# Last layer of a four-layer graph network: shift and weights issued earlier, value projections later, other PSUM banks, output block by block

## The chip, the cores and the metric

The kernel runs on one core of a Trainium2 chip. The metric is the device time of one execution in microseconds (us). The kernel is written engine by engine: TensorE (PE, matmuls), VectorE (DVE), ScalarE (ACT), GpSimd (POOL) and SyncE (SP, which issues the transfers) each run their own list of instructions in order, and wait on semaphores for one another.

## The reference

Four layers, each `x = x + layer(relu(layernorm(x)))`, over 1354 nodes of 256 features with one adjacency matrix. Only the last layer is touched:

```python
def _L3_gnn_ref(x, S, W, U):
    n = x.shape[0]
    S = S + jnp.eye(n, dtype=S.dtype)
    h = x @ W
    scores = h @ U @ h.T
    mask = S > 0
    scores = jnp.where(mask, scores, -jnp.inf)
    att = jax.nn.softmax(scores, axis=-1)
    att = att * mask.astype(att.dtype)
    S_tilde = S * att
    return S_tilde @ h
```

## The kernel before

The 1354 nodes make 11 blocks of 128 rows (the last has 74). Scores are held transposed: for a **group** of output nodes (512, 512 and 330 columns wide; blocks 0 to 3, 4 to 7, 8 to 10) there is one **tile** for each of the 11 blocks j of source nodes, so the layer has 33 tiles, numbered n = 11 * group + j. Each tile passes through this pipeline:

1. `score(n)` on PE: six matmuls (hi*hi, lo*hi, hi*lo, for two halves of the features) into one of two score banks (4, 5). Lines L252 to L254, called from L1327.
2. `add3(n)` on DVE (L1204): mask and score into the SBUF slot of the tile; this frees the score bank. `score(n)` waits for `add3(n-2)`.
3. `running(n)` on DVE (L830, L833): elementwise extreme over the 11 tiles of the group.
4. Once a group: `turn_max` on PE (L1351, transposes of the running extreme into a bank of `B3.shifts`), `top` on DVE (L812, reduction), `spread_max` on PE (L1360, the result spread over the partitions, in the same bank).
5. `shift(n)` on DVE (L841): the slot minus the spread extreme. It can't start before `spread_max` of its group.
6. `exp3(n)` on ACT (L733): exponential in place. For the first tile of a group a second exponential of the same slot goes to `total` first (L732).
7. `times_s(n)` on DVE (L1212): product with the adjacency tile into `w_ring`, a ring of three; it waits until tile n-3 has been aggregated.
8. `add_total(n)` on POOL (L400): sums the exponentials into `total`.
9. `aggregate3(n)` on PE (L1656): for each output block of the group one fp32 matmul of the weights with `v3`, accumulated over 11 tiles in a bank of its own (`B3.sums`, banks 0 to 3 for each group). Each shows as two matmul records, so a tile is 8 records (6 in the last group).
10. Once a group: `add_up` on PE (L1666, the column sums of `total`, into the shift bank), then `out3` on DVE (L1220 reciprocals, one for each block; L1224 scale and add to `x_sb`), then the transfer of each block to DRAM (L304, SP's queue, one for each block).

The value projections `values(b)` (PE, also L252 to L254, 256 columns) fill banks 1 and 2 and are copied to `v3` by ACT (L447). They have to be through before banks 1 and 2 take sums.

The order is written out by hand in loops over a step s. On PE, step s has `score(s)`, then `turn_max` at s = 11, 22, 33 and `spread_max` at 12, 23, 34, then `aggregate3(s - 15)`, then `add_up` at 25, 36, 47. `values` 0 to 7 are in steps 0 to 7, `values(8)` ahead of `make_t(2)` in step 9, 9 and 10 in step 10. On DVE step s has `top` (12, 23, 34), `out3` (26, 37), `add3(s)`, `shift(s - 13)`, `running(s)`, `times_s(s - 14)`; `out3(2)` comes behind the loop. `aggregate3` waits, at tiles 11 and 22, until `out3` of the group ahead has read all its sum banks (L1654 wait on `x_add[3]`).

Of the kernel before, what the change touches and what calls it, by code (L numbers as in the profile page):

```python
# [27 lines left out]
SLOTS3 = 18  # L28
RING = 3
# [19 lines left out]

def item_bank(kind, b):  # L50
    return ITEM_BANKS[ITEMS.index((kind, b))]
# [11 lines left out]
TURNED = [[2, 4, 1, 0] + [2, 4] * 3 + [2], [3] * NB, [7, 3] * 3 + [7] * 5, [3, 4] * 4 + [3, 0, 3]]  # L63
XB_BANKS, XA_BANKS = [4, 5, 6, 7], [0, 1, 2, 3]
# [8 lines left out]
def graph_layers_kernel(nc, x, adjT, wq, wk, wvT, wsa, wgcn, w2, w3, w3T, u3T, asa, cols, rws, eye, out):  # L73
    with ExitStack() as ctx:
# [160 lines left out]
        eye_add, w_set, tot_add, tot_mm = sem("eye_add"), sem("w_set"), sem("tot_add"), sem("tot_mm")  # L235
# [171 lines left out]
        def _(act):  # L407
# [300 lines left out]
            for s in range(NB):  # L708
# [31 lines left out]
        def _(dve):  # L740
# [452 lines left out]
            def add3(n):  # L1193
# [6 lines left out]
                if n >= SLOTS3:  # L1200
                    k = n - SLOTS3
                    dve.wait_ge(w_set, k + 1)
                    wait(dve, tot_add, 10 * (k // NB) + k % NB)
# [22 lines left out]

# [17 lines left out]
            for s in range(NB, NT + LAG - 1):  # L1244
                for gi in range(NG):
                    if s == NB * gi + 12:
                        top(gi, 1, ALU.min)
                    if gi < 2 and s == NB * gi + 26:
                        out3(gi)
                if s < NT:  # L1250
                    add3(s)
                if 13 <= s < NT + 13:
                    shift(s - 13, 1)
                if s < NT:
                    running(s, 1, ALU.min)
                if s >= 14:
                    times_s(s - 14)
# [4 lines left out]
        def _(pe):  # L1262
# [78 lines left out]
            def turn_max(gi, a):  # L1341
# [3 lines left out]
                if gi == 2:  # L1345
                    pe.wait_ge(s_sub[a], NB)
                    if a:
                        pe.wait_ge(rinv_set[1], PER)
# [295 lines left out]
            def aggregate3(n):  # L1644
# [7 lines left out]
                if n % NB == 0:  # L1652
                    wait(pe, x_add[3], last_of(gi - 1) if gi else 0)
                for b in blocks(gi):  # L1654
                    mine = slice((b % PER) * P, (b % PER) * P + rows(b))
                    ins = pe.matmul(ps[0:rows(b), B3.sums[b % PER], 0:D], w_ring[0:k, n % RING, mine], v3[0:k, j, :],  # L1656
                                    start=(j == 0), stop=(j == NB - 1))
                ins.then_inc(agg[1], 1)

            def add_up(gi):  # L1660

                pe.wait_ge(tot_add, 10 * (gi + 1))
                pe.wait_ge(s_sub[1], NB * (gi + 1))
                for b in blocks(gi):
                    k = b % PER
                    ins = pe.matmul(ps[0:rows(b), B3.shifts[gi % 2], k:k + 1],  # L1666
# [3 lines left out]
            for s in range(NT + LAG):  # L1670
# [11 lines left out]
                if s == 9:  # L1682
                    values(8, 1)
                    make_t(2, 1)
                if s == 10:
                    values(9, 1)
                    values(10, 1)
                for gi in range(NG):
                    if s == NB * gi + 11:
# [47 lines left out]
```

## Time and profile before

| | us |
|---|---|
| median of 3 runs | 442.11 |
| lowest, highest | 441.32, 442.44 |
| profiled execution | 442.61 |
| span of its instructions | 440.8 |
| PE busy | 409.3 (93%) |
| DVE busy | 325.4 (74%) |
| ACT busy | 217.4 (49%) |
| POOL busy | 88.5 (20%) |

The span runs from the first to the last instruction; 1.8 us of the profiled time lie outside it. Busy shares are averages over the whole kernel. The last layer's scores begin at about 313 us of the span, and its last transfer ends it. In the profile's tables "issue" is time in which an engine waited for nothing that the profile shows, and PEclk is the clock granted to TensorE, where 1.00 is 2.4 GHz and 0.50 is 1.2 GHz.

### The profile page before, as it was taken

The numbers are of one execution on the slowest core, as the hardware profiler recorded it, in microseconds if no ns is written. First come the engines' busy times: TensorE is split into PE (matmuls) and PEld (weight loads), VectorE is DVE, ScalarE is ACT, GpSimd is POOL, SyncE is SP. The second block draws the span as 40 slices with busy tenths as digits, with TensorE's granted clock in tenths as the row PEclk, the third lists the DMA queues.
The fourth block names the chain that finished last, engine by engine and source line by source line (L and its number), as shares of the span: only waits on it lengthen the run. The fifth ranks groups of instructions, "written<-read, shape, count | busy, mean of one in ns | idle before, by whom it ended". The sixth has DMA issues, their size and how long they took to land.

```text
span 440.8 us, 7365 instructions
## 1 busy us (share of the span) xinstructions
PE 409.3 (93%) x2556; PEld 363.2 (82%) x2556; DVE 325.4 (74%) x749; ACT 217.4 (49%) x446; POOL 88.5 (20%) x105
## 2 busy tenths in 40 slices
PE   8999999999998979999999998898799899999795
PEld 7788789999897969999999767797588788978674
DVE  5899798899865649879989361675467778768872
ACT  2342999955784657876867723124132212212230
POOL 1280000001101324220311020022000033424452
PEclk9999999999999999999999999899699999989989
DMA  8991000000000010000000000000000000010010
GB/s 258 381 372 43 1 1 1 1 0 2 1 1 1 1 49 1 2 0 3 1 0 1 1 1 0 1 1 1 0 1 1 0 0 1 1 49 1 5 45 31
DMA packets 10301, 13.96 MB, mean 32 GB/s; under 512 B 645, under 2 KB 7193, under 8 KB 10265
## 3 DMA queue, kind: packets, MB, share of 16 engines
q1 hardware_dynamic: 10264, 13.49, 9.0%
q8 instruction: 21, 0.34, 0.3%
q14 instruction: 16, 0.12, 0.1%
HBM read 12.10 MB, written 1.39 MB: 31 GB/s over the span
## 4 chain that ended last, share of the span: by engine, by line
PE 75%; DVE 15%; issue 6%; ACT 2%; POOL 0%; DVEq 0%; ACTq 0%; POOLq 0%
PE ps L1656 12%; PE ps L1378 9%; PE ps L1373 8%; PE ps L1374 8%; PE ps L252 6%; PE ps L254 6%; PE ps L253 6%; PE ps L1299 6%; PE ps L1612 4%; PE ps L1613 3%; PE ps L1269 2%; DVE m_sb L833 2%; PE ps L1397 1%; DVE s_sb L803 1%; PE ps L1565 1%
## 5 line engine op out<-in xcount | busy, mean ns | idle before, releaser
L1373 PE MATMUL ps<-v_hi,p_hi 128*128 128x258 f32 (+3 forms) x242 | 64.8, 298 | 1.1 <-DVE x_sb L859 0.7
L1656 PE MATMUL ps<-v,w_ring 128*128 128x256 f32 (+3 forms) x242 | 59.1, 395 | 4.8 <-DVE x_sb L1224 3.2
L1374 PE MATMUL ps<-v_lo,p_hi 128*128 128x258 f32 (+3 forms) x242 | 61.1, 282 | 0.0
L1656 PEld LDWEIGHTS ps<-v,w_ring 128*128 128x128 f32 (+3 forms) x242 | 45.9, 193 | 13.4 <-issue 3.7
L252 PE MATMUL ps<-mid_hi,big_hi 128*128 128x512 f32 (+2 forms) x132 | 54.0, 409 | 1.8 <-DVE big_lo L771 1.0
L253 PE MATMUL ps<-mid_lo,big_hi 128*128 128x512 f32 (+2 forms) x132 | 49.2, 373 | 0.0
L254 PE MATMUL ps<-mid_hi,big_lo 128*128 128x512 f32 (+2 forms) x132 | 49.1, 372 | 0.0
L319 POOL TENSOR_TENSOR mr_all<-mr_all,mhalf 128x4 f32<-128x4 f32 (+1 forms) x12 | 12.8, 1066 | 175.4 <-DVE mr_all L765 175.4
L400 POOL TENSOR_TENSOR total<-total,s_sb 128x512 f32<-128x512 f32 (+3 forms) x27 | 30.8, 1140 | 83.9 <-DVE w_ring L1212 83.9
L1373 PEld LDWEIGHTS ps<-v_hi,p_hi 128*128 128x128 f32 (+3 forms) x242 | 44.7, 185 | 3.5 <-ACT p_hi L453 1.6
L1374 PEld LDWEIGHTS ps<-v_lo,p_hi 128*128 128x128 f32 (+3 forms) x242 | 44.7, 185 | 0.5
L733 ACT ACTIVATE s_sb<-s_sb 128x512 f32<-128x512 f32 (+3 forms) x30 | 17.2, 574 | 50.8 <-DVE s_sb L841 50.8
L1378 PE MATMUL ps<-v_hi,p_lo 128*128 128x258 f32 (+3 forms) x242 | 40.4, 285 | 1.7 <-DVE p_lo L847 1.7
L841 DVE TENSOR_TENSOR s_sb<-s_sb,ps 128x512 f32<-128x512 f32 (+3 forms) x63 | 38.5, 611 | 0.0
L1378 PEld LDWEIGHTS ps<-v_hi,p_lo 128*128 128x128 f32 (+3 forms) x242 | 32.5, 185 | 2.8 <-DVE p_lo L847 2.5
L1204 DVE SCALAR_TENSOR_TENSOR s_sb<-adjT_sb,ps 128x512 f32<-128x512 f32 (+3 forms) x30 | 18.5, 618 | 21.9 <-PE ps L254 21.8
L833 DVE TENSOR_TENSOR m_sb<-m_sb,s_sb 128x512 f32<-128x512 f32 (+3 forms) x51 | 32.7, 640 | 0.6
L1373 PE MATMUL ps<-big_hi,mid_hi 128*128 128x258 f32 (+3 forms) x121 | 31.3, 290 | 1.9 <-ACT mid_hi L561 1.9
L356 POOL TENSOR_TENSOR mid_lo<-adjT_sb,mid_hi 128x512 fp32r<-128x512 f32 (+2 forms) x16 | 19.8, 1238 | 57.8 <-ACT mid_hi L561 57.8
L1374 PE MATMUL ps<-big_lo,mid_hi 128*128 128x258 f32 (+3 forms) x121 | 30.3, 282 | 0.0
L415 ACT ACTIVATE z_buf<-x_sb,mr_all 128x256 f32<-128x256 f32 x40 | 22.4, 591 | 14.7 <-POOL mr_all L322 14.7
L570 ACT ACTIVATE p_hi<-s_sb,minus_r 128x512 fp32r<-128x512 f32 (+3 forms) x33 | 22.2, 672 | 14.5 <-DVE s_sb L1023 7.4
(172 smaller groups left out, 984.7 us busy)
## 6 DMA issues: line engine op xcount, KB each, us to landing
adjT_sb<-in_adjT_dram SPq DMA_DIRECT2D x1, 2816.0 KB, 16.6
adjT_sb<-in_adjT_dram SPq DMA_DIRECT2D x3, 768.0 KB, 10.0
adjT_sb<-in_adjT_dram SPq DMA_DIRECT2D x1, 1815.0 KB, 20.9
out_dram<-x_sb SPq DMA_DIRECT2D x10, 128.0 KB
x_sb<-in_x_dram SPq DMA_DIRECT2D x2, 512.0 KB, 4.6
adjT_sb<-in_adjT_dram SPq DMA_DIRECT2D x1, 512.0 KB, 11.6
rows_sb<-in_rows_dram SPq DMA_DIRECT2D x1, 385.0 KB, 11.2
s_sb<-in_wq_dram SPq DMA_DIRECT2D x1, 256.0 KB, 3.9
```

The source lines that it names most:

```text
L252: eng.matmul(out_ap, lhs[0], rhs[0], start=first, stop=False)
L253: eng.matmul(out_ap, lhs[0], rhs[1], start=False, stop=False)
L254: return eng.matmul(out_ap, lhs[1], rhs[0], start=False, stop=last)
L400: pool.tensor_tensor(r, r, slot3(n), ALU.add).then_inc(tot_add, 1)
L415: act.activation(z_buf[:, b % 4, :], x_sb[:, b, :], ACT.Identity, bias=mr_all[:, b, 0:1], scale=mr_all[:, b, 1:2]).then_inc(zd, 1)
L833: dve.tensor_tensor(m, m, mine(n), op).then_inc(s_max[a], 1)
L841: dve.tensor_tensor(mine(n), mine(n), ps[0:rows(j), bank, 0:CW[gi]], ALU.subtract).then_inc(s_sub[a], 1)
L1299: ins = pe.matmul(out_ap, h_mid[:, b, c, 0:rows(b)], w[:, c, 0:n], start=(c == 0), stop=(last and c == C - 1))
L1373: pe.matmul(out_ap, left_[0][0:k, n % RING, mine], right_[0][0:k, j, 0:cols_], start=(j == 0), stop=False)
L1374: pe.matmul(out_ap, left_[0][0:k, n % RING, mine], right_[1][0:k, j, 0:cols_], start=False, stop=False)
L1378: ins = pe.matmul(ps[0:rows(b), banks[b % PER], 0:cols_], left_[1][0:k, n % RING, mine], right_[0][0:k, j, 0:cols_], start=False, stop=(j ...
L1656: ins = pe.matmul(ps[0:rows(b), B3.sums[b % PER], 0:D], w_ring[0:k, n % RING, mine], v3[0:k, j, :], start=(j == 0), stop=(j == NB - 1))
```

## The change

The order of the last layer's instructions is rewritten from step 9 on; the arithmetic is the same.

- **Value projections**: `make_t(2)` directly behind `score(9)`; `values(8)` between `turn_max(0)` and `spread_max(0)` in step 11, `values(9)` in step 12, `values(10)` in step 13, all behind the step's score. ACT copies them out alternating with `exp3(0)` and `exp3(1)`.
- **Shorter lags**: `shift(n)` in step n + 11 for the first group, n + 12 for the others (before: n + 13); `times_s(n)` one step later, `aggregate3(n)` two. So n + 13 and n + 14 for `aggregate3`, before n + 15. From step 22 on DVE's order in a step is `add3`, `running`, `times_s`, `shift`; up to there it stays `add3`, `shift`, `running`, `times_s`. At steps 11 and 12 it is written out.
- **Banks**: sums of the third group in banks 4, 5 and 7 (`SUMS3`) in place of 0 to 2. The column sums of `total` go to columns 256 and up of bank 3 in place of the shift bank. The third group's first aggregation waits for all scores and all shifts of the second group, no longer for `out3(1)`. The second group's first aggregation waits for `out3(0)` one block at a time.
- **Group ends**: `add_up(0)` behind `aggregate3(10)` in step 23, with no aggregation in step 24; `add_up(1)` behind `aggregate3(21)` in step 35. DVE does `times_s(11)` and `out3(0)` at the head of step 24, `out3(1)` at the head of step 37. `out3` has one reciprocal for the group.
- **Last output**: in `aggregate3(32)` the column sums come behind the first block's matmul, and `out3(2)` takes each block when its own matmul is done.
- **ACT**: `exp3` does the in-place exponential first; for the first tile of a group a copy of the result goes to `total`, behind a wait for it.

```diff
+LAG3 = 14
+def shift_step(n):
+    return n + (11 if n < NB else 12)
+def tiles_at(s, after):
+    return [n for n in range(NT) if shift_step(n) + after == s]
+SUMS3 = [[0, 1, 2, 3], [0, 1, 2, 3], [4, 5, 7]]
+TOTALS_BANK = 3
...
                 act.wait_ge(s_sub[1], n + 1)
+                act.activation(slot3(n), slot3(n), ACT.Exp, scale=-1.0 / TINY).then_inc(pf[1], 1)
                 if j == 0:
                     wait(act, tot_mm, gi - 1)
-                    act.activation(total[0:rows(j), gi % 2, 0:CW[gi]], slot3(n), ACT.Exp, scale=-1.0 / TINY)
-                act.activation(slot3(n), slot3(n), ACT.Exp, scale=-1.0 / TINY).then_inc(pf[1], 1)
-            for n in range(NT):
+                    act.wait_ge(pf[1], n + 1)
+                    act.activation(total[0:rows(j), gi % 2, 0:CW[gi]], slot3(n), ACT.Copy)
+            for b in range(8, NB):
+                values(b, 1)
+                exp3(b - 8)
+            for n in range(3, NT):
                 exp3(n)
...
             def out3(gi):
                 dve.wait_ge(tot_mm, gi + 1)
-                dve.wait_ge(agg[1], NB * (gi + 1))
+                if gi < 2:
+                    dve.wait_ge(agg[1], NB * (gi + 1))
+                b0, b1 = blocks(gi)[0], last_of(gi)
+                dve.reciprocal(rinv[:, b0:b1], ps[:, TOTALS_BANK, D:D + b1 - b0]).then_inc(rinv_set[1], 1)
+                dve.wait_ge(rinv_set[1], gi + 1)
                 for b in blocks(gi):
-                    r, bank = rows(b), B3.shifts[gi % 2]
-                    dve.reciprocal(rinv[0:r, b:b + 1], ps[0:r, bank, b % PER:b % PER + 1]).then_inc(rinv_set[1], 1)
-                for b in blocks(gi):
-                    r, bank = rows(b), B3.sums[b % PER]
-                    dve.wait_ge(rinv_set[1], b + 1)
+                    r, bank = rows(b), SUMS3[gi][b % PER]
+                    if gi == 2:
+                        dve.wait_ge(last_sum, b % PER + 1)
...
-            for s in range(NB, NT + LAG - 1):
-                for gi in range(NG):
-                    if s == NB * gi + 12:
+            add3(11)
+            top(0, 1, ALU.min)
+            shift(0, 1)
+            shift(1, 1)
+            add3(12)
+            times_s(0)
+            running(12, 1, ALU.min)
+            for s in range(13, NT + LAG3 - 1):
+                for gi in range(1, NG):
+                    if s == NB * gi + (12 if gi == 1 else 11):
                         top(gi, 1, ALU.min)
-                    if gi < 2 and s == NB * gi + 26:
-                        out3(gi)
+                if s == 24:
+                    times_s(11)
+                    out3(0)
+                if s == 37:
+                    out3(1)
                 if s < NT:
                     add3(s)
-                if 13 <= s < NT + 13:
-                    shift(s - 13, 1)
+                if s < 22:
+                    for n in tiles_at(s, 0):
+                        shift(n, 1)
                 if s < NT:
                     running(s, 1, ALU.min)
-                if s >= 14:
-                    times_s(s - 14)
+                for n in tiles_at(s, 1):
+                    if n != 11:
+                        times_s(n)
+                if s >= 22:
+                    for n in tiles_at(s, 0):
+                        shift(n, 1)
             out3(2)
...
-                if n % NB == 0:
-                    wait(pe, x_add[3], last_of(gi - 1) if gi else 0)
+                if n == 2 * NB:
+                    pe.wait_ge(s_add[1], NT)
+                    pe.wait_ge(s_sub[1], 2 * NB)
                 for b in blocks(gi):
+                    if n == NB:
+                        pe.wait_ge(x_add[3], b - PER + 1)
...
+                    if n == NT - 1:
+                        ins.then_inc(last_sum, 1)
+                        if b == 2 * PER:
+                            add_up(2)
...
                 if s == 9:
-                    values(8, 1)
                     make_t(2, 1)
-                if s == 10:
-                    values(9, 1)
-                    values(10, 1)
-                for gi in range(NG):
-                    if s == NB * gi + 11:
-                        if gi < 2:
-                            pe.wait_ge(t_lo[1], 2 * NG)
-                        turn_max(gi, 1)
-                    if s == NB * gi + 12:
-                        spread_max(gi, 1)
-                if s >= LAG:
-                    aggregate3(s - LAG)
-                for gi in range(NG):
-                    if s == NB * gi + 25:
-                        add_up(gi)
+                if s == 11:
+                    pe.wait_ge(t_lo[1], 2 * NG)
+                    turn_max(0, 1)
+                    values(8, 1)
+                    spread_max(0, 1)
+                if 12 <= s < 14:
+                    values(s - 3, 1)
...
+                for n in tiles_at(s, 2):
+                    aggregate3(n)
+                    if n == NB - 1:
+                        add_up(0)
+                    if n == 2 * NB - 1:
+                        add_up(1)
```

## Rows read from the trace of the kernel before

**Rows 1.** Who PE waited for from 330 us on (total, times, longest).
```profile
PE ps L1656 <- DVE x_sb L1224: 3.2, 2, 2.1
PE ps L1656 <- DVE w_ring L1212: 1.6, 1, 1.6
PE ps L1360 <- DVE mx L812: 0.6, 1, 0.6
```
**Rows 2.** Busy time of each engine by stretch, granted clock, DMA share, GB/s.
```profile
core 0: us, PE busy (x) PEld busy (x) DVE busy (x) ACT busy (x) POOL busy (x), PEclk, DMA share, GB/s
343.20:352.80 9.60, 8.04 (x40) 6.26 (x38) 7.18 (x13) 2.17 (x4) 0.00 (x0) 1.00 0.00 0
388.00:391.00 3.00, 3.00 (x9) 2.44 (x9) 1.75 (x4) 0.63 (x1) 1.12 (x1) 0.53 0.40 132
...
419.00:423.00 4.00, 3.92 (x11) 2.99 (x12) 3.46 (x7) 1.44 (x3) 2.10 (x3) 0.59 0.33 106
423.00:435.00 12.00, 12.00 (x58) 9.69 (x57) 6.17 (x13) 2.88 (x6) 6.75 (x8) 1.00 0.00 0
```
**Rows 3.** Timeline of PE, steps 9 to 12: start, us, operation.
```profile
338.56 0.32 PE L252 MATMUL ps<-big_hi,wa_hi 128*128 128x330 f32 x1
...
340.38 0.40 PE L252 MATMUL ps<-mid_hi,big_hi 128*74 128x512 f32 x1
...
341.79 0.28 PE L252 MATMUL ps<-wb_hi,big_hi 128*128 128x256 f32 x1
...
343.21 0.39 PE L252 MATMUL ps<-mid_hi,big_hi 128*128 128x512 f32 x1
...
344.61 0.60 PE L1351 MATMUL ps<-ident,m_sb 128*128 128x128 f32 x4
344.96 0.48 PE L252 MATMUL ps<-mid_hi,big_hi 128*128 128x512 f32 x1
```
**Rows 4.** Chain that ended last, in order of time: start, us, what.
```profile
352.82 1.99 PE ps L1656 x8
...
356.21 1.73 PE ps L1656 x8
...
384.98 0.80 PE ps L1666 x8
...
387.88 3.48 PE ps L1656 x8
...
392.43 1.73 PE ps L1656 x8
...
405.49 0.17 PE ps L254
...
416.19 0.80 PE ps L1666 x8
417.02 0.36 DVE rinv L1220 x4
...
419.08 16.07 PE ps L1656 x66
435.15 0.49 PE ps L1666 x6
435.66 0.29 DVE rinv L1220 x3
...
436.74 0.39 DVE x_sb L1224
```
**Rows 5.** Timeline of DVE: one step of group 0, then the tail.
```profile
346.65 0.69 DVE L1204 SCALAR_TENSOR_TENSOR s_sb<-adjT_sb,ps 128x512 f32<-128x512 f32 x1 [0.56 <-PE ps L254]
347.37 0.69 DVE L830 TENSOR_TENSOR m_sb<-s_sb 128x512 f32<-128x512 f32 x1
...
419.26 0.50 DVE L1212 TENSOR_TENSOR w_ring<-s_sb,adjT_sb 128x330 f32<-128x330 f32 x1
419.67 0.49 DVE L841 TENSOR_TENSOR s_sb<-s_sb,ps 128x330 f32<-128x330 f32 x1
```
**Rows 6.** Timeline of ACT: a value copy, exponentials of both widths.
```profile
343.41 0.38 ACT L447 ACTIVATE v<-ps 74x256 f32<-74x256 f32 x1 [0.32 <-PE ps L254]
...
354.00 0.63 ACT L733 ACTIVATE s_sb<-s_sb 128x512 f32<-128x512 f32 x1 [1.77 <-DVE s_sb L841]
...
420.20 0.48 ACT L733 ACTIVATE s_sb<-s_sb 128x330 f32<-128x330 f32 x1 [0.34 <-DVE s_sb L841]
```
**Rows 7.** Timeline of POOL: the last addition into `total`.
```profile
432.13 0.88 POOL L400 TENSOR_TENSOR total<-total,s_sb 74x330 f32<-74x330 f32 x1 [0.43 <-DVE w_ring L1212]
```

More of the change, by code:

```diff
@@ L234, in graph_layers_kernel @@
         p2_mm, h2hi, h2lo, mask2, agg2 = (sem(n) for n in ("p2_mm", "h2hi", "h2lo", "mask2", "agg2"))
-        eye_add, w_set, tot_add, tot_mm = sem("eye_add"), sem("w_set"), sem("tot_add"), sem("tot_mm")
+        eye_add, w_set, tot_add, tot_mm, last_sum = (sem(n) for n in ("eye_add", "w_set", "tot_add", "tot_mm", "last_sum"))
         def wait(eng, s, value):
@@ L1202, in add3 @@
                     dve.wait_ge(w_set, k + 1)
-                    wait(dve, tot_add, 10 * (k // NB) + k % NB)
+                    wait(dve, tot_add, 10 * (k // NB) + max(k % NB, 1))
                 dve.scalar_tensor_tensor(out=slot3(n), in0=adj_tile(n), scalar=0.0,
@@ L1651, in aggregate3 @@
                     h_done(pe, 3, NB)
-                if n % NB == 0:
-                    wait(pe, x_add[3], last_of(gi - 1) if gi else 0)
+                if n == 2 * NB:
+                    pe.wait_ge(s_add[1], NT)
+                    pe.wait_ge(s_sub[1], 2 * NB)
                 for b in blocks(gi):
+                    if n == NB:
+                        pe.wait_ge(x_add[3], b - PER + 1)
                     mine = slice((b % PER) * P, (b % PER) * P + rows(b))
-                    ins = pe.matmul(ps[0:rows(b), B3.sums[b % PER], 0:D], w_ring[0:k, n % RING, mine], v3[0:k, j, :],
+                    ins = pe.matmul(ps[0:rows(b), SUMS3[gi][b % PER], 0:D], w_ring[0:k, n % RING, mine], v3[0:k, j, :],
                                     start=(j == 0), stop=(j == NB - 1))
-                ins.then_inc(agg[1], 1)
+                    if n == NT - 1:
+                        ins.then_inc(last_sum, 1)
+                        if b == 2 * PER:
+                            add_up(2)
+                if n < NT - 1:
+                    ins.then_inc(agg[1], 1)
             def add_up(gi):
                 pe.wait_ge(tot_add, 10 * (gi + 1))
-                pe.wait_ge(s_sub[1], NB * (gi + 1))
+                if gi:
+                    pe.wait_ge(rinv_set[1], gi)
                 for b in blocks(gi):
                     k = b % PER
-                    ins = pe.matmul(ps[0:rows(b), B3.shifts[gi % 2], k:k + 1],
+                    ins = pe.matmul(ps[0:rows(b), TOTALS_BANK, D + k:D + k + 1],
                                     total[:, gi % 2, k * P:k * P + rows(b)], ones[:, 0:1], start=True, stop=True)
                 ins.then_inc(tot_mm, 1)
-            for s in range(NT + LAG):
+            for s in range(NT + LAG3):
                 if 6 <= s <= 8:
@@ L1682, in _ @@
                 if s == 9:
+                    make_t(2, 1)
+                if s == 11:
+                    pe.wait_ge(t_lo[1], 2 * NG)
+                    turn_max(0, 1)
                     values(8, 1)
[L1684 to L1687, printed above, removed]
-                for gi in range(NG):
-                    if s == NB * gi + 11:
-                        if gi < 2:
-                            pe.wait_ge(t_lo[1], 2 * NG)
-                        turn_max(gi, 1)
-                    if s == NB * gi + 12:
-                        spread_max(gi, 1)
-                if s >= LAG:
-                    aggregate3(s - LAG)
-                for gi in range(NG):
-                    if s == NB * gi + 25:
-                        add_up(gi)
+                    spread_max(0, 1)
+                if 12 <= s < 14:
+                    values(s - 3, 1)
+                if s == 22:
+                    turn_max(1, 1)
+                if s == 23:
+                    spread_max(1, 1)
+                if s == 33:
+                    turn_max(2, 1)
+                if s == 34:
+                    spread_max(2, 1)
+                for n in tiles_at(s, 2):
[4 more added lines that the diff above has]
+                        add_up(1)
 _INS = ["x", "adjT", "wq", "wk", "wvT", "wsa", "wgcn", "w2", "w3", "w3T", "u3T", "asa", "cols", "rows", "eye"]
```

2 lines of the change are left out of this document (removed).

## The prediction

> **What bounds the kernel now.** I read the busy shares first: PE is busy 93% of the span, so only time in which PE stands still or runs slowly can be won without removing matmuls, and this change removes none (the last layer's scores, aggregations, transposes and projections are all still there). Then the list of whom PE waited for in the last layer [rows 1]: 3.2 us on `out3` in two waits (ahead of tiles 11 and 22), 1.6 us on the first `times_s`, 0.6 us on `top`. Then the chain that ended last [rows 4], which is PE nearly throughout, so that excess can be read as actual time minus work at the usual pace. Last the granted clock by stretch [rows 2]: it is 1.00 (2.4 GHz) except behind those two waits, 0.53 from 388 to 391 and 0.59 from 419 to 423, which is the 1.2 GHz level for most of them. So each of the two `out3` waits costs about twice what the list of waits shows.
>
> **Pace of the pieces**, from start to start on PE [rows 3] and from the chain [rows 4]. `score` 1.40 us at 512 columns (343.21 to 344.61); `make_t(2)` 1.82 (338.56 to 340.38), which is twelve matmuls of 330 columns, 0.152 each, so a `score` of 330 columns, six of them, is 0.92 with its first one's start. Two `values` 1.42 (341.79 to 343.21), so 0.71 each. Four transposes 0.44, three 0.33 by proportion. An aggregation 1.73 with four blocks and 1.29 with three (three quarters). `add_up` 0.80, and 0.49 for the last. On DVE, one operation after another starts after 0.60 at 512 and 0.41 at 330 columns [rows 5]; an operation that needs the result of the one directly ahead starts after 0.72 at 512 (346.65 to 347.37), so I take 0.53 at 330. Between engines: 0.20 from the last score matmul's slot to the DVE or ACT instruction that reads it (343.21 to 343.41) [rows 3, 6], 0.03 between DVE and ACT, 0.05 from DVE to PE (times as the chain has them).
>
> **Part 1, front of the layer: 0.65 us won.** Before, the first aggregation starts at 352.82 with scores 0 to 15 issued. New, on the same clock: `score(9)` from 336.45, `make_t(2)` to 339.66, scores 10 and 11 to 342.46. `turn_max(0)` has to wait for `running(10)`: score 10 ends at 341.07, DVE starts at 341.27, dependent `running` 0.72 later, its result at 342.68; 0.3 us of wait. `values(8)` to 343.87 covers most of `top`, which ends at 344.03; 0.2 us of wait; `spread_max` to 344.50, `score(12)` to 345.90, `values(9)` to 346.62, `score(13)` to 348.02, `values(10)` to 348.74. Aggregation 0 needs `values(10)` in SBUF: ACT starts 0.20 later and takes 0.38 [rows 6], so 349.38 and a wait of 0.64. Its `times_s(0)` is done by 347.4 (`shift(0)` 344.70, exponential 345.41 to 346.04, `times_s` behind `add3(12)` at 346.70) and `exp3(1)` in front of the ACT copy ends at 347.8, so neither is late. Before, less two scores: 352.82 - 2.79 = 350.03. Won 0.65: the wait of 1.7 us is replaced by three that add up to 1.1. The bounds are 1.7 (no new wait) and 0 (each a third of a microsecond longer). The copy to `total` in place of the exponential costs the same 0.6 us on an ACT that is idle most of the time; the in-place exponential coming first takes 0.6 us from the path of tiles 0, 11 and 22.
>
> **Steady steps: nothing.** PE takes 3.12 us a step (1.40 + 1.73) against 2.4 on DVE (four operations), and `times_s` still stands one step ahead of its aggregation. From step 22 PE has 2.65 and DVE 0.53 + 0.41 + 0.60 + 0.60 = 2.14. The reordering there leaves `times_s(n)` behind `add3` and `running`, 1.4 us behind its `shift`; the exponential needs 0.71 + 0.66 = 1.37 (0.63 of it the exponential) [rows 6]. If DVE comes late, all of the 2.14 has to fit, and it does.
>
> **Part 2, group 0 to group 1: 2.3 us won.** Before: from `add_up(0)` at 384.98 to tile 12's aggregation at 392.43 PE does 0.80 + 1.73 + 2 x 0.92 = 4.37 us of work in 7.45, an excess of 3.08 [rows 4]. New: `add_up(0)` is followed by scores 24 and 25 (1.84 us), which cover `out3(0)`: reciprocal from +0.18, first block's `x_add` at about +0.8, then one every 0.41, and PE asks for them from +1.84, one every 0.43. That wait is gone. What is late next is `times_s(12)`. Queued on DVE behind `out3(0)`, with t = 0 where PE starts aggregation 11: `add3(24)` 0.2, `running(24)` 0.7, `shift(12)` 1.1, `add3(25)` 1.7, `running(25)` 2.25, `times_s(12)` 2.65, result 3.4. PE has aggregation 11 and score 26 in front: 2.65. So a new wait of 0.74, once; a step later DVE has caught up. Net 3.08 - 0.74 = 2.34. Bounds for that wait: 0 and 1.1.
>
> **Part 3, group 1 to the end of the aggregations: 3.5 us won.** Before, from score 32's last matmul at 405.66 (405.49 + 0.17) to 435.15 are 29.49 us. The work is aggregations 17 to 21, 5 x 1.73 = 8.65; two sets of three transposes 0.66; `add_up(1)` 0.80; 11 x 1.295 = 14.24; together 24.35. Excess 5.14: 1.2 up to `add_up(1)` (`turn_max(2)` and `spread_max(2)` wait, since `top(2)` stands behind a `times_s` that waits for the ring), 2.09 for `out3(1)`, 1.83 of slow clock behind it. New: sums in banks 4, 5, 7 take the `out3(1)` wait away, and `top(2)` stands ahead of its step's `times_s`. I laid the steps out from score 32's end as 0: aggregations 18 from 0, 19 from 2.06, 20 from 4.12, 21 from 5.85, `add_up(1)` 7.58, tile 22 from 8.38, 23 from 9.67; `top(2)` at 2.3, `times_s(21)` ready at 5.81, `times_s(22)` at 7.3. No wait up to there, one by a hair. Then two new ones. `out3(1)` sits ahead of `times_s(24)` on DVE: 8.99 + 0.18 + 4 x 0.41 = 10.82, ready at 11.37, PE free at 10.97: 0.40. And from there on `shift(n)` comes directly ahead of `times_s(n)` with nothing between, so the loop shift to exponential (0.49 + 0.03), exponential to `times_s` (0.48 + 0.03), `times_s` to next shift (0.41) takes 1.45 us a tile against PE's 1.295: 8 tiles x 0.155 = 1.24. Net 5.14 - 1.64 = 3.50. Bounds: the loop is 1.29 (PE's, hidden) to 1.6, so 4.7 to 2.3.
>
> **Part 4, the end: 0.5 us won.** Before, start of aggregation 32 to the end of the last `x_add`: 1.29 + 0.16 + 0.49 + 0.02 + 1.47 = 3.43 (433.70 to 437.13) [rows 4]. New, the column sums stand behind the first block's matmul and wait for POOL's last addition: `times_s(32)` is 0.05 older than aggregation 32, POOL starts 0.13 later and needs 0.88 [rows 7], so `add_up(2)` starts at 1.0 in place of 0.43. Then 0.49, two blocks 0.86, drain 0.2, last `x_add` 0.4: 2.97. Won 0.46; without the POOL wait it would be 1.0. Before, POOL was hidden since PE was three tiles behind; the exponential loop takes that cover away. The three last transfers come as before, 0.4 us apart, and the last needs the same 3.7 us from `x_add` to the end of the span.
>
> **Sum.** 0.65 + 2.34 + 3.50 + 0.46 = 6.95 us. Against the profiled 442.61 (which is 0.5 above the median): 435.7; against the median 442.11: 435.2. I take 435.4.
>
> **The clock.** The trace has three waits of PE of like size and two outcomes: 1.7 us ahead of 352.82 left the clock at 1.00 (343.20 to 352.80, PE busy 8.04 of 9.60) [rows 2], while 1.08 us ahead of 387.88 and 2.1 us ahead of 419.08 were each followed by about 3 us at 1.2 GHz; both of these stood close behind an `add_up`, eight matmuls of one column. The Trainium skill, page "TensorE: Matmul & The Clock Gate", Part 1, says that the activity window is free-running and does not reset with the work, so that how many matmuls run cold differs between runs of one kernel. By that a wait of given length can go either way, and the two outcomes here agree. The sum above has no drop left.
>
> **Rivals.** (A) One drop of the clock stays, behind the 0.74 us wait at tile 12 or behind `add_up(1)` and the 0.40 us wait. It costs what the chain shows [rows 4]: 3.48 - 1.73 = 1.75 for one aggregation plus 0.2 for the score behind it. Gives 437.3. For: the same neighbourhood as before. Against: waits are a third of the old ones, with dense scores between. Chance 0.2. (B) DVE and ACT hand over sooner than I took, or DVE stays ahead, so that the tail is PE's: 1.24 + 0.5 more, 433.7. Against: both durations are in the rows. Chance 0.12. (C) Both drops stay and the front wins nothing: 435.4 + 3.7 + 0.65 = 439.8, or with the loop at 1.6 another 1.2, 441.0. Chance 0.07. (D) Slower: in the tail PE stops briefly at each tile; if that takes the clock to 1.2 GHz and holds it there, a tile costs 2.59 in place of 1.45, for 10 tiles 11.4 us: 446.8. It decides at about 6 such tiles. Against: before, at 1.2 GHz the clock came back within 3.5 us under full load, and a slow PE is a busy PE. Chance 0.03. (E) The change doesn't act: aggregation 22 still waits, since one of its new conditions is as late as `out3(1)` was. By the layout all scores and shifts of group 1 are done 2.7 us ahead. Chance 0.03, about 439.
>
> **How the numbers follow.** My forecast has 0.55. The range leaves out (D) and most of (C): 433.3 (B with a little more) to 438.9 (A and a lost front). A measurement of this kernel can tell about 0.3%, 1.3 us, from no change. Faster by more than that holds for the forecast, A, B, E and most of C: 0.93; within: 0.04; slower: D and what I overlooked, 0.03.
>
> **What would show it.** Right: no wait of L1656 on `x_sb` L1224; granted clock 1.00 from 385 to the end of the aggregations; last layer's aggregations 25 to 32 at 1.45 us each, with DVE's L1212 waiting for ACT's L733; a wait of L1656 on `w_ring` near tile 12 of 0.7 us and of about 0.6 us of L1666 on POOL in the last tile. Wrong: tiles at 1.29 us (then the loop is shorter than I took), a clock of 0.5 anywhere in the layer behind its start, or a first aggregation later than 349.4.

## The result

The changed kernel takes 437.42 us (median of 4 runs, 435.35 to 438.10); beside it the kernel before took 442.27 (median of 4, 441.32 to 443.16). These medians differ by 4.9 us, 1.1%; the ratio on record is 0.987 with a 95% interval of 0.984 to 0.991, so the kernel is faster. Ratios leave out the few slow executions, those over 1.5% above the fastest of their kernel; medians take in all. Over all later comparisons the kernel before had a median of 443.1 (23 runs in the largest of them), and a second set of the changed kernel gave 437.33 and a ratio of 0.986, which is 5.8 us. The forecast was 435.4, 6.7 us less than before, in a range of 433.3 to 438.9.

| | before | after |
|---|---|---|
| median, us | 442.27 | 437.42 |
| profiled execution, us | 442.61 | 437.66 |
| span, us | 440.8 | 435.9 |
| start of score 9 | 336.45 | 337.61 |
| start of score 9 to the end of the last `x_add` | 100.68 | 94.57 |

The last row is the part that the change touches. Its start is worked out from the first matmul of `make_t(2)`, less one score (1.40) and, where `values(8)` stands between them, less another 0.71. In this part the change wins 6.11 us; 1.16 us of it are lost ahead of score 9, in code that it doesn't touch.

Who PE and DVE waited for in the last layer of the changed kernel (total, times, longest; PEld is the load of a matmul's stationary operand; L1686 is the aggregation, L1702 `add_up`, L1223 `times_s`, L737 the exponential, L411 POOL's addition):

```profile
DVE w_ring L1223 <- ACT s_sb L737: 7.1, 13, 0.7
...
PEld ps L1686 <- DVE w_ring L1223: 4.5, 11, 0.8
...
PE ps L1686 <- DVE w_ring L1223: 0.8, 2, 0.5
...
PE ps L1702 <- POOL total L411: 0.3, 1, 0.3
```

The row of the `out3` waits in [rows 1] is gone: no aggregation waits for `x_sb` any more. In its place stand `times_s` waiting 13 times for the exponential, and the aggregation's weight loads waiting 11 times for `times_s`. Busy time and granted clock by stretch (columns as in [rows 2]):

```profile
343.00:351.00 8.00, 7.23 (x43) 5.76 (x42) 6.76 (x12) 3.01 (x7) 0.00 (x0) 1.00 0.01 2
384.00:390.00 6.00, 5.52 (x33) 5.04 (x34) 5.81 (x13) 1.31 (x3) 0.19 (x1) 1.00 0.26 87
390.00:405.00 15.00, 15.00 (x80) 13.69 (x80) 13.16 (x25) 3.79 (x6) 7.52 (x7) 1.00 0.00 1
405.00:417.00 12.00, 12.00 (x64) 10.03 (x62) 9.52 (x20) 3.81 (x7) 5.97 (x5) 1.00 0.04 13
417.00:430.00 13.00, 12.44 (x52) 8.11 (x51) 7.56 (x17) 3.83 (x8) 7.97 (x9) 1.00 0.09 31
```

The clock is 1.00 throughout these stretches; [rows 2] had 0.53 and 0.59 behind the two waits. The chain that ended last, at the places of [rows 4]:

```profile
350.78 1.97 PE ps L1686 x8
...
383.88 0.80 PE ps L1702 x8
...
388.99 0.69 DVE w_ring L1223
389.73 1.99 PE ps L1686 x8
...
413.54 0.79 PE ps L1702 x8
414.32 1.42 PE ps L1686 x6
...
418.64 0.51 DVE s_sb L852
419.17 0.49 ACT s_sb L737
419.82 0.28 issue
420.10 0.50 DVE s_sb L852
420.62 0.49 ACT s_sb L737
...
427.55 0.90 POOL total L411
...
429.93 0.75 PE ps L1702 x6
430.70 0.19 DVE rinv L1231
430.92 0.88 DVE x_sb L1237 x2
```

Behind `add_up(1)` at 413.54 the next aggregation follows at once, where [rows 4] has 2.1 us of waiting for `out3`. Then the chain leaves PE and runs around the loop of `shift` (L852), exponential (L737) and `times_s`, 1.46 us a turn (418.64 to 420.10), and ends over POOL.

### The profile page after: what moved, and what is told of

Read it like the earlier page. It is cut to its first block, busy times and chain, and to the rows that moved or that the text cites. A ratio compares the mean times of both kernels' runs of the same rounds, so it can differ in the third digit from the quotient of the medians.

```text
span 435.9 us, 7356 instructions
## 1 busy us (share of the span) xinstructions
PE 409.0 (94%) x2556; PEld 360.6 (83%) x2556; DVE 323.3 (74%) x741; ACT 217.5 (50%) x446; POOL 87.9 (20%) x105
## 3 DMA queue, kind: packets, MB, share of 16 engines
q1 hardware_dynamic: 10264, 13.49, 9.0%
## 4 chain that ended last, share of the span: by engine, by line
PE 73%; DVE 15%; issue 6%; ACT 3%; POOL 1%; DVEq 0%; POOLq 0%; ACTq 0%
PE ps L1686 9%; PE ps L1405 9%; PE ps L1400 8%; PE ps L1401 8%; PE ps L263 6%; PE ps L265 6%; PE ps L264 6%; PE ps L1328 6%; PE ps L1639 4%; PE ps L1640 3%; PE ps L1298 2%; DVE m_sb L844 2%; PE ps L1424 2%; DVE s_sb L814 2%; PE ps L1592 1%
## 5 line engine op out<-in xcount | busy, mean ns | idle before, releaser
L1686 PE MATMUL ps<-v,w_ring 128*128 128x256 f32 (+3 forms) x242 | 58.0, 385 | 1.3 <-DVE w_ring L1223 0.8
L1686 PEld LDWEIGHTS ps<-v,w_ring 128*128 128x128 f32 (+3 forms) x242 | 43.2, 185 | 11.1 <-DVE w_ring L1223 4.5
L411 POOL TENSOR_TENSOR total<-total,s_sb 128x512 f32<-128x512 f32 (+3 forms) x27 | 30.5, 1131 | 80.3 <-DVE w_ring L1223 80.3
L737 ACT ACTIVATE s_sb<-s_sb 128x512 f32<-128x512 f32 (+3 forms) x30 | 17.3, 575 | 54.0 <-DVE s_sb L852 54.0
L852 DVE TENSOR_TENSOR s_sb<-s_sb,ps 128x512 f32<-128x512 f32 (+3 forms) x63 | 38.5, 612 | 0.8 <-PE ps L1387 0.7
L1034 DVE SCALAR_TENSOR_TENSOR s_sb<-s_sb,sx 128x512 f32<-128x512 f32 (+3 forms) x33 | 28.4, 859 | 1.2
```

The source lines that it names most:

```text
L411: pool.tensor_tensor(r, r, slot3(n), ALU.add).then_inc(tot_add, 1)
L852: dve.tensor_tensor(mine(n), mine(n), ps[0:rows(j), bank, 0:CW[gi]], ALU.subtract).then_inc(s_sub[a], 1)
L1034: dve.scalar_tensor_tensor(out=sum1(n), in0=left[0:rows(j), gi, 0:CW[gi]], scalar=sx[0:rows(j), j, 0:1], in1=sum1(n), op0=ALU.add, op1=ALU ...
L1686: ins = pe.matmul(ps[0:rows(b), SUMS3[gi][b % PER], 0:D], w_ring[0:k, n % RING, mine], v3[0:k, j, :], start=(j == 0), stop=(j == NB - 1))
```

## Experiments

All are read in two ways: by time, and by their own trace from the start of score 9 to the end of the last `x_add` (100.68 us before, 94.57 after). The second is what a wait or a slow clock in the last layer changes and nothing else, since the time ahead of score 9 differs between executions. How far a trace repeats can be read from the front: from score 9 to the first aggregation it is 16.34 to 16.37 us in all five kernels with the order of before, and 13.17 or 13.18 in the seven that have the changed front. By time the variants of the changed kernel can't be told from one another; what is said of them rests on one trace each. Each ratio is taken against executions of the kernel before that ran beside that kernel. Line numbers in rows of an experiment are its own. Where an expectation counts from the first aggregation, the changed kernel and its variants have two scores (2.79 us) more in that stretch than the kernel before and its variants.

| kernel | score 9 at | score 9 to last `x_add` | median us (runs) | ratio to before |
|---|---|---|---|---|
| before | 336.45 | 100.68 | 443.1 (23) | |
| changed | 337.61 | 94.57 | 437.42 (4) | 0.987 (0.984 to 0.991) |
| changed, again | 337.72 | 94.56 | 437.33 (4) | 0.986 (0.982 to 0.989) |
| before, banks alone | 336.77 | 98.83 | 440.98 (7) | 0.994 (0.991 to 0.996) |
| before, gap alone | 335.29 | 99.48 | 441.67 (12) | 0.997 (0.995 to 1.000) |
| before, waits filled | 338.79 | 99.23 | 442.61 (12) | 0.998 (0.996 to 1.001) |
| before, waits filled, half | 336.20 | 97.29 | 439.98 (12) | 0.993 (0.991 to 0.995) |
| changed, values back | 337.30 | 94.51 | 437.06 (2) | 0.987 (0.982 to 0.992) |
| changed, end back | 336.83 | 94.88 | 436.52 (2) | 0.986 (0.981 to 0.991) |
| changed, whole wait | 336.29 | 94.54 | 436.75 (2) | 0.986 (0.980 to 0.992) |
| changed, tail shift | 337.37 | 92.98 | 435.86 (5) | 0.983 (0.979 to 0.987) |
| best | 343.91 | 92.07 | 435.09 (6) | 0.981 (0.978 to 0.985) |
| best2 | 337.80 | 91.80 | 434.17 (4) | 0.981 (0.977 to 0.984) |

In the profiled execution of "best" the clock was at 0.50 from 260 to 270 us, ahead of the last layer, and its score 9 comes late; in its last layer the clock is 1.00.

### The changed kernel again

> The changed kernel once more, nothing altered: a second trace of it and more times. Theory: the last layer comes out the same to 0.1 us (first aggregation 13.17 us behind the start of score 9, tiles 25 to 32 at 1.46 us, last x_add 26.3 us behind the end of score 32), and what differs between executions lies ahead of score 9, which started at 337.61 us in the profiled execution of the changed kernel and at 336.45 in that of before, in code that neither touches. Rival: the 1.16 us ahead of score 9 belong to the change; then score 9 starts at 337.6 again.

Score 9 at 337.72, the same part 94.56 us: the last layer repeats to 0.01 us. By the one number named in the expectation the rival would stand. But all thirteen kernels have the same instructions ahead of step 9, and without "best" their score 9 starts between 335.29 and 338.79 in the five with the order of before and between 336.29 and 337.80 in the seven with the changed order. The 1.16 us lie well inside that, so I take them for scatter ahead of the last layer; twelve single traces don't rule out a small share of the change. The clock ahead of the last layer differs between executions too. Two stretches of the kernel before:

```profile
250.00:260.00 10.00, 8.97 (x52) 6.71 (x51) 7.47 (x27) 4.70 (x13) 2.81 (x6) 1.00 0.01 2
280.00:290.00 10.00, 10.00 (x77) 10.00 (x77) 8.42 (x28) 0.00 (x0) 0.74 (x1) 0.88 0.01 2
```

The same two of the changed kernel:

```profile
250.00:260.00 10.00, 8.99 (x44) 6.92 (x43) 6.86 (x25) 4.30 (x12) 2.08 (x4) 0.83 0.00 0
280.00:290.00 10.00, 8.74 (x73) 8.59 (x73) 9.22 (x29) 1.42 (x3) 0.00 (x0) 1.00 0.01 2
```

One execution has its slow clock at 280 us, the other at 250. That isn't where the 1.16 us come from, though: the changed kernel is up to 4.9 us behind at 255 us and back to 0.8 at 283. The 0.8 are there by 11 us of the span, and 0.3 to 0.4 more come between 312 and 319.

### Which part won it: banks alone

```diff
+SUMS3 = [[0, 1, 2, 3], [0, 1, 2, 3], [4, 5, 7]]
+TOTALS_BANK = 3
...
-                if n % NB == 0:
-                    wait(pe, x_add[3], last_of(gi - 1) if gi else 0)
+                if n == NB:
+                    wait(pe, x_add[3], last_of(gi - 1))
+                if n == 2 * NB:
+                    pe.wait_ge(s_add[1], NT)
+                    pe.wait_ge(s_sub[1], 2 * NB)
...
```

`out3`, `aggregate3` and `add_up` use these banks, and `add_up` waits for the reciprocals of the group ahead.

> The kernel before with the banks of the change alone: third group's sums in banks 4, 5, 7, totals in bank 3, aggregation 22 free of out3(1), nothing else moved. Theory (the wait is in DVE's order as much as in the bank): aggregation 22 starts 2.1 us earlier, at 417.0, but times_s(23) is queued behind out3(1) and is ready only at 419.8, so aggregation 23 waits 1.5 us and the clock falls as before: 0.5 us less than before, 441.6. Rival (the bank was the cause): the wait of 2.1 and the slow clock of 1.8 both go, 438.2.

1.85 us won in the trace, between the two expectations, and by time 0.6% (0.4 to 0.9). PE's timeline around aggregations 22 and 23 (start, us, engine, line, operation, idle before):

```profile
416.34 0.95 PE L1671 MATMUL ps<-ones,total 128*128 128x1 f32 x8
417.15 1.54 PE L1661 MATMUL ps<-v,w_ring 128*128 128x256 f32 x6
420.12 4.05 PE L1661 MATMUL ps<-v,w_ring 128*128 128x256 f32 x17 [1.43 <-DVE w_ring L1214]
```

The wait moved as the theory had it: aggregation 22 starts at once, and aggregation 23 waits 1.4 us since its `times_s(23)` is queued behind `out3(1)`. The bank by itself is worth 0.5 us there. What the theory missed is the clock: this time it stayed at 1.00 (2.88 of 4.00 us busy from 419 to 423, PEclk 1.00), behind a wait that is longer than the 1.07 us ahead of aggregation 11 in the same execution, behind which it fell (0.61 from 388 to 391). That is the other 1.3 us.

### Which part won it: the gap ahead of aggregation 11

```diff
-                if s >= LAG:
-                    aggregate3(s - LAG)
-                for gi in range(NG):
-                    if s == NB * gi + 25:
-                        add_up(gi)
+                n = s - LAG if s < NB + LAG else s - LAG - 1
+                if s >= LAG and s != NB + LAG:
+                    aggregate3(n)
+                    if n % NB == NB - 1:
+                        add_up(n // NB)
```

> The kernel before with one thing of the change: between add_up(0) and aggregation 11 PE does two scores (26 and 27) in place of one; aggregations 11 to 32 come one step later, lags on DVE, banks and the rest as before. Theory (a second score of 0.92 us is what covers out3(0), and with the wait goes the slow clock behind it): PE asks for x_add at 1.84 us behind add_up, all four blocks stand 1.97 behind it, so the wait falls from 1.08 to 0.15 and the clock stays at 1.00: 0.93 + 1.92 = 2.85 us less from the first aggregation to the last x_add, 81.5 in place of 84.31, and 440.3 in all; tile 22 still waits 2.1 and is slow behind it. Rival (out3(0) then delays times_s(12), as in the changed kernel, by 0.7): 82.2. Rival (the clock falls anyway): 83.4.

1.20 us won over the whole part, not 2.85. Up to `add_up(1)` it went as the theory says: from the first aggregation to `add_up(1)` 60.78 us (351.63 to 412.41) against 63.37 (352.82 to 416.19) before, 2.6 won; the wait for `x_sb` at aggregation 11 is 0.17 and the clock stays up. Behind the other wait, which is as long as before, 1.4 us of it are lost again:

```profile
415.31 17.49 PE ps L1656 x66
```

The same 66 records took 16.07 us in [rows 4]. The clock by single microseconds in this execution:

```profile
414.00:415.00 1.00, 0.00 (x0) 0.00 (x0) 1.00 (x3) 0.00 (x0) 0.00 (x0) 0.78 0.13 46
415.00:416.00 1.00, 0.69 (x2) 0.64 (x3) 1.00 (x4) 0.40 (x1) 0.00 (x0) 0.50 0.81 267
...
420.00:421.00 1.00, 1.00 (x4) 0.69 (x3) 0.13 (x1) 0.00 (x0) 0.00 (x0) 0.50 0.00 0
421.00:422.00 1.00, 1.00 (x5) 0.80 (x4) 0.79 (x2) 0.18 (x1) 0.54 (x1) 0.80 0.00 0
```

It was at 1.2 GHz for 7 us, under aggregations that ran without a break once they had started, against 3.3 us in the execution of [rows 2]. So what this variant wins in its first half is the wait and the slow clock together; the run doesn't part them.

### What the slow clock costs: waits filled with matmuls of no use

The second run has 4 and 8 matmuls in place of 8 and 16.

```diff
+                if n == NB:
+                    pe.wait_ge(s_add[1], 2 * NB + 4)
+                if n in (NB, 2 * NB):
+                    for _ in range(8 if n == NB else 16):
+                        pe.matmul(ps[:, 5 if n == NB else 4, 0:P], ident[:, :], ones[:, :], start=True, stop=True)
                 if n % NB == 0:
                     wait(pe, x_add[3], last_of(gi - 1) if gi else 0)
```

> The kernel before with matmuls of no use, 8 ahead of aggregation 11 and 16 ahead of aggregation 22, each 128 columns into a score bank that is free there; every wait is kept. Theory (the stillness of PE is what takes the clock to 1.2 GHz behind the out3 waits, and that costs as much as the waits): the clock stays at 1.00, aggregation 11 takes 1.75 in place of 3.48, tiles 22 to 24 take 1.3 each; from the first aggregation to the last x_add 80.7 us in place of 84.31, and 438.5 in all. Rival (the clock falls for another reason, such as what PE did before): 84.3 and 442.3; or it falls at one of the two: 82.5.

The clock stayed at 1.00 in both places, and aggregation 11 took 1.73 us. But I had sized the filling wrongly: a matmul of 128 fp32 columns takes 0.224 us, twice what I had assumed. Eight of them take 1.8 us in a wait of 1.08, sixteen 3.6 us in a wait of 2.1. What was left of the 3.7 us is 1.45 in the trace, and by time no difference can be told.

> As waits_filled with half the matmuls of no use: 4 ahead of aggregation 11 (0.9 us, the wait is 1.08) and 8 ahead of aggregation 22 (1.8 us, the wait is 2.09). waits_filled kept the clock at 1.00 but its matmuls took 0.224 us each, 0.7 and 1.6 us more than the waits that they fill. Theory: the clock stays at 1.00 with these too and nothing is added, so all of the slow clock's 3.75 us shows: 80.6 us from the first aggregation to the last x_add, 438.6 in all. Rival (the short stillness that is left is enough): one or both drops come back, 82.4 or 84.3.

With half of them:

```profile
387.00:390.00 3.00, 2.91 (x17) 2.51 (x17) 2.49 (x6) 0.63 (x1) 0.37 (x1) 1.00 0.53 175
416.00:419.00 3.00, 2.88 (x17) 2.39 (x17) 3.00 (x7) 0.96 (x2) 0.89 (x1) 1.00 0.53 175
```

3.39 us won with every wait of the kernel before in place, 0.7% by time (0.5 to 0.9). That the clock held isn't an accident of one trace: the mean clock over the whole execution was 0.987 or 0.991 in all 12 executions of this kernel, and 0.983 or less in 22 of the 23 of the kernel before that ran beside it. So of the excess at the two group ends about 3.4 us were the slow clock and 3.2 the waits. `add_up` by itself doesn't take the clock down, since it is still there; PE has to stand still as well. Whether standing still suffices isn't shown: every fall in the last layer had an `add_up` at most one score ahead of the wait. Of the two longer waits behind which the clock stayed up, the one ahead of the first aggregation (1.6 us) has no `add_up` near it, and that in banks alone (1.43) has an aggregation in between.

### The front: value projections back

`values(8)` to `values(10)` stand where they were before, on PE and on ACT; the lags are as changed.

> The changed kernel with the value projections 8 to 10, and ACT's copies of them, where they were before; lags, banks and the rest as changed. Read from score 9's start to the first aggregation, which is 16.37 us in the kernel before (13.58 less two scores) and 13.17 in the changed one. Theory (the front's gain comes from the shorter lag, the moved projections only trade one wait for another): PE waits 0.9 us for top between turn_max and spread_max with nothing over it, but no longer 0.35 for running(10) nor 0.5 to 0.8 for the copy of projection 10, so 13.0 to 13.3. Rival (the projections are what covers the waits): 13.9, the 0.9 us on top.

94.51 against 94.57 us, and 13.11 from score 9 to the first aggregation against 13.17: no difference worth naming. The wait is where the theory puts it:

```profile
345.44 0.60 PE L1379 MATMUL ps<-ident,m_sb 128*128 128x128 f32 x4
346.98 0.65 PE L1388 MATMUL ps<-ident,mx 128*128 128x128 f32 x4 [0.94 <-DVE mx L824]
```

PE stands 0.94 us between the two sets of transposes with no projection to do there, and gets it back at `turn_max` and at the first aggregation, where it no longer waits. Moving the projections is worth nothing. What remains for the front's gain is the shorter lag with the new order on DVE and ACT in steps 11 and 12; these two weren't tried apart.

### The end: sums behind all blocks again

```diff
-                    if n == NT - 1:
-                        ins.then_inc(last_sum, 1)
-                        if b == 2 * PER:
-                            add_up(2)
-                if n < NT - 1:
-                    ins.then_inc(agg[1], 1)
+                ins.then_inc(agg[1], 1)
+                if n == NT - 1:
+                    add_up(2)
...
```

`out3(2)` waits for the whole aggregation again.

> The changed kernel with the end as before: all three blocks' matmuls of tile 32, then the column sums, then out3(2) with no wait a block. Read from the start of tile 32's aggregation to the end of the last x_add: 3.21 us in the changed kernel, 3.43 in that of before. Theory: the sums then wait for POOL less (0.43 + 0.86 = 1.29 of cover against 1.0 needed, so not at all), and the end takes 3.4: 0.2 us longer than the changed kernel. Rival (block by block is worth the 0.86 of two blocks): 0.9 longer.

0.31 us longer over the whole part. In this trace tile 32's weights are ready at 428.10 and the last `x_add` ends at 431.71, 3.61 us; in the changed kernel 428.92 and 432.18, 3.26. So the last edit is worth 0.3 us, near what the theory gives and far from the 0.86 of two blocks: with the sums moved forward PE waits for POOL instead.

### The wait by block at aggregation 11

One wait for all four blocks of `out3(0)` in place of one a block.

> The changed kernel with aggregation 11 waiting for all four blocks of out3(0) before its first matmul, in place of one at a time. Theory (two scores cover out3(0) but for its last block): in the changed kernel aggregation 11 starts at 386.44 and the fourth x_add stands at 386.59, so PE waits 0.2 us, and that comes off the wait at tile 12 behind it: no change, 81.4 us from the first aggregation to the last x_add. Rival (the wait by block carries the gain at this place): 0.5 us or more longer, or the clock falls, 83.3.

94.54 against 94.57 us. Aggregation 11 starts 0.3 later and tile 12 waits 0.3 less. The two scores cover `out3(0)` but for its last block, and what waiting by block wins there is lost again at tile 12.

### The tail: shifts of the third group one step earlier

```diff
+EARLY = range(2 * 11 + 1, 3 * 11)
+def shifts_at(s):
+    return [n for n in range(NT) if shift_step(n) - (n in EARLY) == s]
...
                 if s >= 22:
-                    for n in tiles_at(s, 0):
+                    for n in shifts_at(s):
                         shift(n, 1)
```

> The changed kernel, with the shifts of the third group's tiles but its first one step earlier, nothing else. Theory (the loop shift, exponential, times_s, next shift sets the tail at 0.41 + 0.52 + 0.51 = 1.45 us a tile): with another tile's work between them the tail goes at PE's 1.30, 8 x 0.155 = 1.2 us won; the wait for out3(1) ahead of tile 24 stays (0.4), and PE falls far enough behind DVE that POOL's last addition is covered again, 0.6 won. Together 1.8 us less than the changed kernel, 435.6. Rival (PE itself takes 1.45 a tile in this stretch, or DVE is full): no change, 437.4.

1.59 us won. One tile's `shift` now follows the last at 1.33 us in place of 1.46, PE's pace:

```profile
417.64 0.48 DVE s_sb L857
...
418.97 0.45 DVE s_sb L857
```

and PE's aggregations from tile 22 on run without a break. So the loop was the bound of the tail in the changed kernel, as the theory has it. The total came near the 1.8 expected partly by luck, since two smaller parts of the theory were wrong and made up for each other. The wait at tile 24, which was to stay, went: its `shift` now stands ahead of `out3(1)`. And the wait for POOL, which was to go, stayed: POOL's third last addition took 1.49 us in place of 0.89 and the last `add_up` waited 0.39 for it. The traces of banks alone and of waits filled, half, have the same slow addition (1.48), and in all three DVE's last two `times_s`, which run beside it, take 1.59 together; in the next two kernels they take 2.31 and the addition 0.89. Why it is sometimes the one and sometimes the other that comes out longer stays open.

### A version that beats both

"Best" also makes the second group's shifts but the first one step earlier, and splits `out3(1)`:

```diff
-                if s == 37:
-                    out3(1)
+                if 37 <= s < 41:
+                    out3(1, s - 37)
```

> The changed kernel with three edits of DVE's order: all shifts but tiles 11 and 22 one step earlier from step 23 on, and out3(1) split into one block a step over steps 37 to 40. Theory: no wait of PE left from aggregation 11 to the end, so in addition to the 1.8 us of tail_shift the wait at tile 12 (0.5 to 0.7) and the one at tile 24 (0.4) go: 2.9 us less than the changed kernel, 434.5. Rival: moving the work only moves the wait (shift(12) ahead of times_s(11) delays out3(0)); then no better than tail_shift, 435.6.

2.50 us less than the changed kernel in the same part; `add_up(1)` is followed by 62 records in 13.49 us, ten tiles and a block without a wait. Of the 0.9 us beyond the tail shift 0.8 lie behind `add_up(1)`, where POOL's slow addition is missing here, so the split of `out3(1)` has little to show for itself. The wait at tile 12 stayed (0.5 us): `shift(13)` had taken `shift(12)`'s place in the queue.

> The kernel best with times_s(12) ahead of add3(25) on DVE, in step 24, nothing else. In best the wait at tile 12 stayed at 0.5 to 0.75, since shift(13) took the place of shift(12) in the queue. Theory: times_s(12) is then ready about 0.9 us ahead of PE and the wait goes: from the first aggregation to the last x_add 78.2 us in place of 78.90 (81.40 in the changed kernel, 84.31 before), 434.3 in all. Rival (add3(25), now 0.6 us later, holds up score 27): no change, 78.9.

0.27 us less than "best", not 0.7. Tile 12 waits no more; tile 13 does:

```profile
389.27 1.89 PE L1694 MATMUL ps<-v,w_ring 128*128 128x256 f32 x8
392.29 0.92 PE L1694 MATMUL ps<-v,w_ring 128*128 128x256 f32 x3 [0.21 <-DVE w_ring L1228]
```

`out3(0)` puts 1.8 us on DVE, which has only 0.5 us to spare in a step of 2.65. These orders chose the tile that pays; none of them let all go free. This version is at 434.17 us, ratio 0.981 (0.977 to 0.984) to the kernel before, 3.2 us less than the changed kernel by the medians. By time it can't be told from "best".

## Why the prediction was right, point by point

| step of the prediction | won, predicted | won, measured |
|---|---|---|
| 1 front, score 9 to first aggregation | 0.65 | 0.41 |
| 2 first aggregation to the end of score 32 | 2.34 | 2.28 |
| 3 end of score 32 to the start of aggregation 32 | 3.50 | 3.20 |
| 4 start of aggregation 32 to the last `x_add` | 0.46 | 0.22 |
| sum | 6.95 | 6.11 |

Between the first aggregation and the end of score 32 the changed kernel does two scores (2.79) and one aggregation (1.73) more than the kernel before, and as much less ahead of it and behind it; rows 1 to 3 are evened out for that. The first two waits of the front, from PE's timeline of the changed kernel (score 11 ends at 343.63, the values at 345.16):

```profile
343.98 0.63 PE L1378 MATMUL ps<-ident,m_sb 128*128 128x128 f32 x4 [0.18 <-DVE m_sb L844]
...
345.04 0.28 PE L265 MATMUL ps<-wb_hi,big_lo 128*128 128x256 f32 x1
345.39 0.32 PE L1387 MATMUL ps<-ident,mx 128*128 128x128 f32 x1
```

- **Front.** Right in place, a little small in size. The three new waits are 0.35 (predicted 0.3), 0.23 (0.2) and 0.68 (0.64); each also costs PE about 0.05 to 0.1 to start again, which I had left out. By that one of my own signs of being wrong came up, narrowly: on the clock of the kernel before the first aggregation starts at 349.62 (350.78 less 1.16), and I had named anything later than 349.4. The moved projections, which I had covering part of the waits, cover them but win nothing (values back).
- **Group 0 to 1.** Right. The two scores cover `out3(0)` (gap alone, whole wait), the clock stays up, and `times_s(12)` is late: its aggregation starts at 389.73, 3.29 behind that of tile 11, where 2.65 us of work lie between: 0.64 late, against 0.74. The profile shows 0.48 of it as idle.
- **Group 1 to the end.** Right in mechanism. Tile 24 starts 0.5 us late behind `out3(1)` (0.40 predicted), and from there a tile takes 1.456 us (11.65 for eight) against the 1.45 worked out. The loss that the tail shift showed to be the loop's doing was in the sum. Of the 0.30 by which the part falls short 0.14 are tile 24's; the rest isn't traced to one place.
- **End.** The wait for POOL came (0.53 against 0.57). What follows was the wrong path, and one term of it was mis-sized. I let the last block's matmul set the last `x_add`, but it comes too early; DVE's reciprocal and three `x_add` do, 1.48 us from 430.70 to 432.18. By luck that is as long as the 1.46 that I had summed for the other path. The 0.24 that are missing are the column sums themselves: 0.49 in a stream, which I had taken, but 0.75 behind a wait (429.93 to 430.68).
- **The clock.** The forecast had no drop left, and there was none in the traces of the two executions of this kernel, nor in those of its variants from score 9 to the end of the aggregations. The mean clock of all eight executions was 0.986 or more, that of the kernel before 0.979 in its trace.
- **The time itself.** 435.4 forecast, 437.4 measured. 0.8 us are in the table. The other 1.2 are the frame: I took the profiled execution of before as a base for a part that I didn't model, and the profiled execution of after had its score 9 1.16 us later, most likely scatter. Against the larger set of runs of before (443.1), 5.8 us were won, and the layer's own 6.1 fit that. Rival A (one drop of the clock, 437.3) would give nearly the measured time; the granted clock of 1.00 rules it out. The time alone couldn't have told it from a layer without a drop and with a late start. The measured time lies nearer to A's than to my own forecast, so it is the trace and not the time that speaks for the mechanism.
- **What no run parts.** The shorter lags weren't tried alone; they are given the front's gain since nothing else that was tried explains it. Parts of the change tried on the kernel before are banks alone (1.85) and gap alone (1.20); their shares depend on where the clock fell in that one trace.
- **The other rivals.** B fell with the tail at 1.46 us a tile, C and D with the clock at 1.00, E with the aggregation at 414.32 right behind `add_up(1)`, without a wait.

## What to carry to other kernels

When the bounding engine waits at a group's end, move its own later work between the last step of one group and the first that needs the result, and count what is queued behind the epilogue on the engine that does it: freeing the bank alone only handed the wait to the next tile (0.5 us of 2.1). When a lag is cut by a step, look for a round trip over two engines (here `shift`, exponential, `times_s`) that loses the other tile's work that lay in it: putting one tile's work back between won 1.6 us here. And compare a part of the trace that starts at the edit, not spans: the front scattered by more than most of the edits were worth.

## What the runs showed of the hardware that I had not expected

- Equal waits of PE did not end equally. The clock fell to 1.2 GHz behind 1.08 us in the kernel before and behind 1.07 us in its banks-alone variant, and stayed at 2.4 GHz behind 1.43 us there and behind 1.6 us in the kernel before. The Trainium skill, page "TensorE: Matmul & The Clock Gate", Part 1, says that the activity window is free-running and doesn't reset when a kernel starts. Outcomes that go either way would fit that, but no run here shows the window.
- Time at the slow clock was not constant either: 3.3 us behind tile 22's wait in one execution, 7 us in another (gap alone), with PE at aggregations without a break in both once it had started.
- Matmuls whose results nobody reads kept the clock up. Four and eight of them, 0.9 and 1.8 us in waits of 1.1 and 2.1, were worth 3.4 us.
- PE's work behind a wait takes longer than in a stream: an aggregation 1.97 to 1.99 us against 1.73, the last column sums 0.75 against 0.49, as the chain counts them. From start to start it is less: aggregation 12 of the changed kernel, behind a wait, and 13 start 2.75 us apart, where 2.65 is the pace.
- A POOL addition of 128x330 fp32 took 1.48 or 1.49 us in three traces where 0.89 is usual, beside two `times_s` on DVE that took 1.59 together; in two traces the addition took 0.89 and the two `times_s` 2.31.
